# A decoder block in one kernel: order of TensorE's step (transpositions, product 1, scores, values, product 2), and the moves of a latent copy, its signal, moments and scales

## The reference

```python
c_q = hidden_states @ w_q_down                       # 1024 -> 384
q_nope = (c_q @ w_q_up_nope)...                      # 32 heads x 128
q_rope = _apply_rope((c_q @ w_q_up_rope)...)         # 32 heads x 64
c_kv = hidden_states @ w_kv_down                     # 1024 -> 128
k_rope = _apply_rope((hidden_states @ w_k_rope)...)
q_lat = jnp.einsum('bhsd,hdr->bhsr', q_nope, wuk)
scores = jnp.einsum('bhsr,btr->bhst', q_lat, c_kv) + jnp.einsum('bhsd,btd->bhst', q_rope, k_rope[:, 0])
probs = jax.nn.softmax(masked scores / sqrt(192))
out_lat = jnp.einsum('bhst,btr->bhsr', probs, c_kv)
out = jnp.einsum('bhsr,hdr->bhsd', out_lat, wuv)
return out @ w_out
...
x = x + _L0_attn_ref(_layernorm(x, axis=-1), ...)
x = x + _L0_xattn_ref(_layernorm(x, axis=-1), ctx_4096)
x = x + _L0_ffn_ref(_layernorm(x, axis=-1), ...)
```

## Time and profile before

| | |
|---|---|
| median of the runs | 1904.76 us (1904.56 to 1905.6) |
| the profiled execution | 1904.51 us, its span 1902.7 us |
| TensorE busy | 1895.1 us (100%) |
| VectorE, ScalarE, GpSimd busy | 81%, 62%, 55% of the span |
| chain that ended last | 96% TensorE, 3% VectorE, 1% GpSimd |
| DMA | 393 MB, 207 GB/s on average |

### The profile page before, as it was taken

The page is one execution under the profiler, slowest core; times in us unless marked ns, Lnnn a source line. Parts: engine busy times, 40 slices in busy tenths (PEclk is TensorE's granted clock), DMA queues, the critical chain, the costliest instruction groups (busy, mean ns, idle before and its releaser), DMA issues.

```text
span 1902.7 us, 32230 instructions
## 1 busy us (share of the span) xinstructions
PE 1895.1 (100%) x9920; PEld 1596.3 (84%) x9920; DVE 1548.5 (81%) x3168; ACT 1184.2 (62%) x2904; POOL 1038.3 (55%) x1019
## 2 busy tenths in 40 slices
PE   9999999999999999999999999999999999999999
PEld 7888888888888888888888888888888877888887
DVE  6778888888888888887888778887878889996677
ACT  5457767676758575765565555655656668766441
POOL 5458777787869696965555556555665511000000
PEclk9999999999999999999999999999999999999999
DMA  9839575657474756698747374474738476466645
GB/s 361 331 113 317 136 256 137 248 134 257 130 269 136 237 166 206 196 322 304 206 154 228 87 232 134 158 206 144 221 87 299 134 257 240 199 221 251 231 149 177
DMA packets 328154, 393.27 MB, mean 207 GB/s; under 512 B 271616, under 2 KB 272384, under 8 KB 313088
## 3 DMA queue, kind: packets, MB, share of 16 engines
q1 hardware_dynamic: 328064, 392.21, 63.5%
HBM read 236.46 MB, written 155.71 MB: 206 GB/s over the span
## 4 chain that ended last, share of the span: by engine, by line
PE 96%; DVE 3%; POOL 1%; issue 0%; ACT 0%; DVEq 0%; ACTq 0%; POOLq 0%
PE at_out L1325 11%; PE at_out L1329 10%; PE at_out L1326 10%; PE at_qbank L55 7%; PE at_qbank L57 7%; PE at_qbank L56 7%; PE at_qbank L1649 3%; PE at_score L1286 3%; PE at_score L1649 3%; PE at_score L1289 3%; PE at_turned L1300 2%; PE at_out L1649 2%; PE at_value L55 2%; PE at_value L56 2%; PE at_value L57 2%; PE at_value L1649 2%
## 5 line engine op out<-in xcount | busy, mean ns | idle before, releaser
L2686 DVE TENSOR_TENSOR at_acc<-at_out,at_acc 128x512 f32<-128x512 f32 x640 | 438.8, 689 | 126.8 <-PE at_out L1329 119.5
L2315 POOL TENSOR_TENSOR at_acc<-at_stage,at_acc 128x512 f32<-128x512 f32 x256 | 331.7, 1296 | 174.5 <-ACT at_stage L1791 164.9
L1325 PE MATMUL at_out<-at_wvo,at_val_hi 128*128 128x512 f32 x896 | 365.5, 408 | 1.0 <-ACT at_stage L1791 0.5
L1329 PE MATMUL at_out<-at_wvo,at_val_lo 128*128 128x512 f32 x896 | 351.4, 392 | 0.0
L1326 PE MATMUL at_out<-at_wvo,at_val_hi 128*128 128x512 f32 x896 | 350.0, 391 | 0.0
L1791 ACT ACTIVATE at_stage<-at_out 128x512 f32<-128x512 f32 x256 | 153.3, 599 | 94.4 <-PE at_out L1329 82.2
L1329 PEld LDWEIGHTS at_out<-at_wvo,at_val_lo 128*128 128x128 f32 x896 | 168.1, 188 | 38.6
L1325 PEld LDWEIGHTS at_out<-at_wvo,at_val_hi 128*128 128x128 f32 x896 | 168.7, 188 | 31.8 <-DVE at_acc L2686 5.3
L1326 PEld LDWEIGHTS at_out<-at_wvo,at_val_hi 128*128 128x128 f32 x896 | 169.1, 189 | 25.4
L1832 ACT ACTIVATE at_pT<-at_turned 128x256 fp32r<-128x256 f32 x128 | 49.0, 383 | 226.8 <-PE at_turned L1300 225.9
L1827 ACT ACTIVATE at_probs<-at_probs,at_row_stats 128x128 f32<-128x128 f32 (+1 forms) x512 | 184.0, 361 | 8.9 <-DVE at_row_stats L2633 8.9
(11 more groups left out here) (323 smaller groups left out, 5041.8 us busy)
## 6 DMA issues: line engine op xcount, KB each, us to landing
parts_d<-at_rope_tmp SPq DMA_DIRECT2D x32, 1024.0 KB, 6.9
at_qrope<-parts_d SPq DMA_DIRECT2D x128, 256.0 KB, 4.6
wvo_d<-at_wvo SPq DMA_DIRECT2D x16, 2048.0 KB, 7.5
at_wvo<-wvo_d SPq DMA_DIRECT2D x16, 2048.0 KB, 8.3
ff_w_d<-ff_w SPq DMA_DIRECT2D x21, 1024.0 KB, 6.4
ff_w<-ff_w_d SPq DMA_DIRECT2D x21, 1024.0 KB, 4.8
ab_raw<-in_w_heads SPq DMA_DIRECT2D x32, 576.0 KB, 6.1
wvo_d<-at_wvo SPq DMA_DIRECT2D x16, 1024.0 KB, 10.2
```

The source lines that it names most:

```text
L1325: pe.matmul(out, hi, weight[:, 0], start=start, stop=False, skip_group_check=True)
L1329: pe.matmul(out, lo, weight[:, 0], start=False, stop=True, skip_group_check=True).then_inc(out_ready, 1)
L2315: pool.tensor_tensor(at, stage[group][z][:], at, ALU.add).then_inc(pool_added, 1)
L2686: dve.tensor_tensor(at, outb[FACTORS[name][2]][:], at, ALU.add).then_inc(added, 1)
```

## The change

It changes the order of work on four places, and no operation, size or buffer.

- TensorE's `slot`: the transposition comes first, then P1, then rope scores and the scores against latent keys, then values, then P2. Only where no step s + 2 follows (steps 6 and 7 of the last quad) P2 stays ahead of values.
- `values`: the second batch of the pair before the first.
- `rope_waits` names the steps 1 and 4 of full and switch quads (not step 1 of quad 0). There ScalarE copies the latent ahead of the value sums, and VectorE signals it ahead of the add of P3 instead of behind it.
- Last quad, VectorE: the first half of the moments of cross attention moves from ahead of the values' low part to behind the add of P7, and the scales of the feed-forward part from batch 4 of cross attention to step 6.

```diff
--- before.py
+++ after.py
@@ -658,6 +658,10 @@
         def pool_adds_later(m, s):
 
             return STAGED * (later(m, s) + 1)
+
+        def rope_waits(m, s, kind):
+
+            return s in ROPE_AT and kind in ("full", "switch") and not opens(m, s, 1)
 
         def absorbed(kind, s):
             if kind == "full":
@@ -1308,7 +1312,7 @@
 
                     pe.wait_ge(prep_turn_taken, lo_at["kv", N - 1] + 1)
                 pe.wait_ge(pT_lo_done, STEPS * m + s + 1)
-                for bl in range(2):
+                for bl in (1, 0):
                     cols = batch_cols(s, bl)
                     at = heads_at(bl)
                     ins = three_passes(pe, value[:, at.start * SEQ:at.stop * SEQ], tok[:, c, KV_HI + cols.start:KV_HI + cols.stop],
@@ -1441,9 +1445,6 @@
                 use, t = USE[kind], s + 2
                 if t < end:
                     score_ropes(m, t, group_of(kind, t))
-                if s + 1 < end:
-                    turn(m, s + 1)
-                if t < end:
                     score_rests(m, t, first - AFTER[kind] if t < 4 else first + use[2 * (t // 2) - 3] + 1)
 
             def next_latent(m, s, end, kind, first, ks=range(QT)):
@@ -1469,14 +1470,19 @@
             def slot(m, s, end, kind, first):
 
                 use, part = USE[kind], absorbed(kind, s)
-                sooner = s in ROPE_AT and kind in ("full", "switch") and not opens(m, s, 1)
+                sooner = rope_waits(m, s, kind)
+                if s + 1 < end:
+                    turn(m, s + 1)
+                product_1(m, s, kind, first)
                 next_scores(m, s, end, kind, first)
                 if kind == "last" and s >= 6:
                     cross_scores(s - 6, (0,))
-                product_1(m, s, kind, first)
-                product_2(m, s)
+                if s + 2 >= end:
+                    product_2(m, s)
                 if s + 1 < end:
                     values(m, s + 1, group_of(kind, s + 1))
+                if s + 2 < end:
+                    product_2(m, s)
                 if kind == "last" and s >= 6:
                     cross_scores(s - 6, (1,))
                 product_6(m, s, kind)
@@ -1972,11 +1978,13 @@
                     latent(m, s // 2 + 2, s % 2, use[s])
                 if kind == "last" and s in (2, 3, 5, 6):
                     cross_normalise((2, 3, 5, 6).index(s))
+                if rope_waits(m, s, kind):
+                    latent(m, s // 2 + 2, s % 2, use[s])
                 if s + 1 < end and not is_late(m, s):
                     value_sums(m, s + 1)
                 if s - late_rope in ROPE_AT and end > STEPS:
                     rope(m + 1, ROPE_AT[s - late_rope])
-                if s // 2 + 2 < end // 2 and not (part and what == "B") and not opens(m, s, 1):
+                if s // 2 + 2 < end // 2 and not (part and what == "B") and not opens(m, s, 1) and not rope_waits(m, s, kind):
                     latent(m, s // 2 + 2, s % 2, use[s])
                 if part:
                     if what == "A":
@@ -2789,13 +2797,13 @@
                     add_product(m, s, group, "P5", 1, 1)
                 if kind == "last" and s >= 6:
                     cross_moments(s - 3)
+                    if s == 6:
+                        feed_scales()
                     cross_largest(s - 6)
                 if not of and not opens(m, s):
                     add_product(m, s, group, "P6", 1, 0)
                 if late:
                     add_product(m, s, group, "P7", 1, 1)
-                elif beside is not None:
-                    cross_half_moments(beside, 0)
                 if s + 1 < end and not opens(m, s, 1):
                     direct_values(m, s + 1)
                 if opens(m, s):
@@ -2824,10 +2832,14 @@
                 else:
                     if not of and not opens(m, s):
                         add_product(m, s, group, "P7", 1, 1)
+                    if beside is not None:
+                        cross_half_moments(beside, 0)
+                    if rope_waits(m, s, kind):
+                        latent(m, s // 2 + 2, s % 2, use[s])
                     add_product(m, s, group, "P3", 0, 1)
                     if opens(m, s):
                         rope_keys(N - 1, (2,))
-                    if s // 2 + 2 < end // 2:
+                    if s // 2 + 2 < end // 2 and not rope_waits(m, s, kind):
                         latent(m, s // 2 + 2, s % 2, use[s])
                     add_product(m, s, group, "P4", 1, 0)
                 if beside is not None and not late:
@@ -2882,6 +2894,13 @@
                     of = cr_out_last if (b, n) == (BATCHES - 1, 1) else cr_out[n][:]
                     dve.scalar_tensor_tensor(out=x2_of(b)[:, cols], in0=of, scalar=cr_rtotal[:, b:b + 1],
                                              in1=x1_of(b)[:, cols], op0=ALU.mult, op1=ALU.add).then_inc(cr_summed, 1)
+
+            def feed_scales():
+                dve.wait_ge(ff_const_in, 16 * 4)
+                for l in range(LAYERS - 1):
+                    dve.tensor_scalar(act_scale[:, l, :], row_scale[:], scale[:, l:l + 1], None,
+                                      ALU.mult).then_inc(ff_scales_ready, 1)
+                dve.tensor_scalar(out_scale[:, 0:1], scale[:, 2:3], 2.0, None, ALU.mult).then_inc(ff_scales_ready, 1)
 
             def feed_half_moments(n, h):
                 if n < 8 and h == 0:
@@ -2936,12 +2955,6 @@
                         cross_moments(n)
                     if b == FIRST_TILE - 1:
                         feed_variances(0)
-                    if b == 4:
-                        dve.wait_ge(ff_const_in, 16 * 4)
-                        for l in range(LAYERS - 1):
-                            dve.tensor_scalar(act_scale[:, l, :], row_scale[:], scale[:, l:l + 1], None,
-                                              ALU.mult).then_inc(ff_scales_ready, 1)
-                        dve.tensor_scalar(out_scale[:, 0:1], scale[:, 2:3], 2.0, None, ALU.mult).then_inc(ff_scales_ready, 1)
                     if FIRST_TILE <= b < BATCHES - 1:
                         feed_normalise(b - FIRST_TILE + 1)
                     if b in MOMENTS_BEHIND:
```

## The result

The changed kernel takes 1938.34 us (median of four runs, 1938.19 to 1938.41), the kernel before 1905.05 us beside it: ratio 1.0175, 95% interval 1.0163 to 1.0187. It is slower by 33.3 us, 1.75%. The spans of the profiled executions are 1936.5 and 1902.7 us, both at a granted clock of 1.000.

What follows compares the result with a forecast made beforehand. TensorE, busy 1895.1 of 1902.7 us, was taken as the bound. Terms 6.1, 8.5, 1.4, 11.9, 1.2 and 0.5 made +29.6 on 1904.5, 1934.1, forecast as 1934 us; range 1909 to 1945.

Steps and rivals of the forecast that it cites:

- P4 wait: In plain steps P4 waits for VectorE's add of P7, late through the values' later copy: 0.15 us a step.
- Start 0.17 after the end: On TensorE, a matmul starts 0.17 us after the end of the operation it waits for.
- The order itself: TensorE's step: new neighbours of small matmuls cost 0.03 us a step, 4 us over 127 steps.
- Values against the low parts: Values, 0.67 us earlier, wait for VectorE's low parts: 0.13 behind a rope, 0.38 or 0.14 behind heads, 0.81 in step 1.
- Steps 7 and 0 of full quads: Transpositions' wait costs 0.5 us more, values wait 0.36 in step 0: 0.87, seven times, 6.1 in the sum.
- The latent's signal: Steps 1 and 4 of full and switch quads: the wait before the second rope half goes, 2.4 us less.
- Quad 0, +1.2: Steps 1 to 6 of quad 0, as of each of quads 0 to 6, lengthen by 1.22 us together.
- Last quad, 1.7: Last quad: about +1.2 us net around the moments and 0.5 for its other steps.
- faster: Rival: present waits go and nothing comes late, 1897 us, or 1901 with order cost and half the gain; chance 0.10.
- No P4 wait: Rival: VectorE's delay shrinks below 0.14, only values' and step-0 waits stay: 1924 us, 1915 with those at half; chance 0.16.
- Worse: Rival: transpositions' wait for GpSimd spreads to plain steps, 56 x 0.2 us more, 1946 and up; chance 0.06 (over 1942).

Runs made afterwards that it cites:

- experiment 2: Changed kernel, but ScalarE copies the values and makes their high part ahead of P2's copy: 1922.38 us, ratio 1.0089.
- Experiment 5: Kernel before with only the transposition moved, to stand first in TensorE's step: 1908.67 us, ratio 1.0018.
- experiment 1: Changed kernel, but P2 stands ahead of the values again in every step: 1911.82 us, ratio 1.0036.
- experiment 7: Changed kernel, but ScalarE cuts the rope weights in step 1 behind the copies of the transposed rows: 1934.77 us, ratio 1.0156.
- Experiment 3: Kernel before with only the latent's earlier copy and signal in steps 1 and 4 of full and switch quads: 1902.97 us, ratio 0.9988.
- experiment 9: Changed kernel, but P1 stands behind the scores as it did before: 1937.20 us, ratio 1.0168.
- the later cut: ScalarE's rope-weight cut behind step 1's copies of transposed rows; with signal and moments moves on the kernel before: 1899.10 us, ratio 0.9969.

## Why the prediction was right, and where it was not

The sign, the size (1934 against 1938.3) and the main place of the loss were right. The size is partly luck: the sum holds 4 us for the order that are not there, and without them it would be 1930; the last quad, quad 0 and the P4 wait were too small by more than that. By its own steps:

- **Start 0.17 after the end.** Held in the places tested: P7's add ends at 1051.08, which gives 1051.25 for P4 against a place of 1051.14, and P4 comes out 0.11 late; P5's add ends at 1050.29, which gives 1050.46 for P3 against 1050.37, and P3 comes out 0.08 late.
- **P4 wait, 0.15 a step.** P3 and P4 together measured 0.19. The mechanism (ScalarE's written order puts P2's copy ahead of the values' copies) is shown by experiment 2; in the changed kernel the low part starts at 5.67 where 5.68 was worked out, and the weight loads of P3 and P4 name VectorE's add.
- **The order itself, 0.03 a step, 4 us.** Wrong. Experiment 5 gives 0, and so does the changed kernel once P3's and P4's waits are taken off. One 512-column product a step has the slower first gap behind small matmuls (0.315 instead of 0.235), before and after the change; in experiment 1 two have it, and there the 0.03 appears. Here the Trainium skill's formula for an isolated gap (TensorE: Matmul & The Clock Gate, "Back-to-back issue gap"), in which neighbours have no part, was the better guide to the sum, though not to the single gap: most small ones stand 0.11 apart at 128 and at 64 columns alike. The 0.03 here and the 0.15 above make 0.18 for a measured 0.19, by luck.
- **Values against the low parts.** Step by step in quads 1 to 6, predicted and measured difference: step 1 0.14 and 0.08 (the bracket in the sum comes to 0.20, not to 0.14), step 2 0.30 and 0.32, step 3 0.18 and 0.20, step 4 0.03 and -0.02, step 5 0.15 and 0.06, step 6 0.42 and 0.34. The wait in step 1, predicted 0.81, is 0.77 to 0.79, and experiment 7 takes it down to 0.13 at its cause. Behind a rope 0.13 was predicted, 0.15 measured (9.60 against 9.45). For the step that holds the rope 13.65 was named and 13.53 to 13.56 measured: the wait behind a rope falls in the next step, and the sum counts it once, rightly.
- **Steps 7 and 0 of full quads, 0.87.** The sum was right (10.91 + 10.65 to 11.78 + 10.70 is 0.92), its parts were not. I had 0.5 for the transpositions and 0.36 for the values of step 0. Measured, all on the way from step 7 to step 0: transpositions 0.25 more, values of step 7 0.1 (those of step 0 do not wait), and 0.5 in a place that I had not listed: the first half of the absorbed head in step 7.

Timelines of ScalarE, GpSimd and TensorE in the changed kernel, step 7 of quad 1:

```profile
324.43 0.59 ACT L1845 ACTIVATE at_val_whole<-at_value 128x512 f32<-128x512 f32 x1
325.06 0.53 ACT L1847 ACTIVATE at_val_hi<-at_val_whole 128x384 fp32r<-128x384 f32 x1
325.49 0.30 ACT L1803 ACTIVATE ab_uv_hi<-ab_raw 128x128 fp32r<-128x128 f32 x1
325.69 1.15 ACT L1804 ACTIVATE ab_proj_hi<-ab_raw 128x512 fp32r<-128x512 f32 x2
...
326.81 2.56 POOL L2272 TENSOR_TENSOR ab_low<-ab_raw,ab_proj_hi 128x512 fp32r<-128x512 f32 x2
...
328.23 0.49 PE L55 MATMUL at_qbank<-ab_proj_hi,ab_uv_hi 128*128 128x512 f32 x1 [0.25 <-POOL ab_low L2272]
```

ScalarE's cuts for the head stand behind the copies of the values, which stand behind the copy of P2; the first low part ends near 328.1 and TensorE starts 0.1 to 0.2 later. It comes from P2's late copy like the P4 wait, one engine further, but not from ScalarE's order alone: with the copies exchanged (experiment 2) the list still has 1.1 of the 1.7 us for `ab_low`, as the cuts stand behind both copies, and with P2 back ahead of the values (experiment 1) none. I had costed step 7 only by its last wait, the transposition's, and that one shrank since the new wait comes ahead of it.

- **The latent's signal, 2.4 less.** Experiment 3: 2.3 (1905.25 against 1902.97 in the same comparison); right.
- **Quad 0, +1.2.** Measured 3.3. I had put no cost on the signal at the end of the opening, for which P1 waits where scores used to fill the time. But that is not the main part: undoing it gives back only 0.6 (experiment 9), while exchanging ScalarE's copies gives back 1.9 with P1's wait left as it is (experiment 2). Two other waits of the first two steps show why. The absorbed head of step 0 waits 1.2 for ScalarE's copy `at_qlat` (0.6 before), and the second rope half of step 1 waits 0.6 for the low part of the rope weights; in experiment 2 they wait 0 and 0.1. So most of it is ScalarE's order once more, in a chain that I had not priced.
- **Last quad, 1.7.** Measured 4.3, the largest miss. The steps behind the moments are right (+1.2 for the first five intervals), though the label was not: what waits at the earlier trace rows is P3, for the add of P5, not P5. The late steps were put at 0.5 and cost 3.1. There is no latent between P6 and P7 in them, so P7 meets P2's copy at once.

Timelines of ScalarE and TensorE in the changed kernel, step 4 of the last quad:

```profile
1516.49 0.60 ACT L1797 ACTIVATE at_stage<-at_out 128x512 f32<-128x512 f32 x1 [2.60 <-PE at_out L1333]
...
1516.69 0.39 PE L1333 MATMUL at_out<-at_wvo,at_val_lo 128*128 128x512 f32 x1
1517.14 0.50 PE L1329 MATMUL at_out<-at_wvo,at_val_hi 128*128 128x512 f32 x1
```

P2's copy ends at 1517.09 and P7 is taken at 1517.14, 0.45 behind its neighbour instead of 0.23, with 0.11 more in its own gap. In experiment 1 this wait is absent. The other late waits are P1's for the add of P3, 0.47, 0.47 and 1.05, the last the longest, as in the last step no transposition stands ahead of P1 either: it follows P4 directly. In experiment 1 all three are there and experiment 9 takes them away but for 0.2, so they belong to P1's early place. In step 4, where P1 waits only 0.24, the transposition at the end of the step waits 0.3 for the normalised rows; the transposition's move alone does that (experiment 5: 8.38 instead of 8.11).

Of the rivals, "faster" failed where it was said to: VectorE did not start the low parts earlier behind heads and ropes, and ScalarE's order held the values. "No P4 wait" is experiment 2 in effect, 1922.4 where I had 1924, and near by luck: it took away 16 us where the rival had 9.9, from a kernel 4 slower. "Worse" did not come: the transpositions' wait did not spread to plain steps, whose 9.45 is explained by P3 and P4 alone.

## What to carry to other kernels

When two operations change places on the engine that is the bound, look up in which order the next engines take their results: a copy that stands ahead in ScalarE's list keeps the other one waiting, and the price appears three operations later. An operation placed early is free only if what it needs is early in every kind of step; price each kind (behind a head, behind a rope, first and last steps) by itself, and list every product of the short steps in which there is nothing between producer and consumer. Try the small moves without the large one: here the signal, the moments and one more of their kind (the later cut) gave 0.3% without it, and the first two were hidden under a loss of 1.75%. Read the weight loads beside the matmuls: their rows name a wait that the matmuls' rows swallow.

## What the runs showed of the hardware

- The first 0.11 us of a wait of TensorE appears neither as idle time nor as a later record: the waiting matmul's record starts in its place and the distance to the *next* record grows, 0.31 to 0.34 where 0.227 is normal. Only what goes beyond makes the record late (P3 in step 2 of the last quad: 0.03 late, and 0.335 to the next). The record of the weight load does show it: P4's begins at 1051.14, behind VectorE's add (end 1051.08), instead of with the matmul before (1050.91). The Trainium skill (Perfetto Trace Analysis, "Per-engine timelines") says that the reported start is the start of the data prefetch and that the reported end is computed; the rows agree with the second, with lengths of 0.39 at a distance of 0.227, and no run here shows the first.
- Neighbours change single gaps (a 512-column product behind small ones 0.315 instead of 0.235). Moving them about changed the sum little: 82.2 us for eight steps in experiment 5 as before, and 9.29 instead of 9.26 a step in experiment 1, where two products stand behind small ones.
- The opening, which no experiment was meant to touch, took 133.7 to 134.9 us in different kernels.
